# First expert tile's weights split, rows turned and first two product groups made during self-attention's last tiles

## What is computed

```
x = x + cross_attention(layernorm(x), ctx)        # 16 heads of 32
x = x + self_attention(layernorm(x))              # latent keys and values, rope, 16 heads
x = x + experts(layernorm(x))
experts: w, idx = top_k(xf @ Wr, 2); w = softmax(w)
         h = xf @ W1[e]; g = xf @ W3[e]; y = (silu(h) * g) @ W2[e]     # e of 8, hidden 768
         out = sum over the two chosen experts of w * y
```

## Time and profile before

| | us |
|---|---|
| median of three runs (lowest, highest) | 1528.22 (1528.01, 1528.5) |
| the profiled execution's own time | 1529.74 |
| its span, first to last instruction | 1528.0 |
| PE busy | 1446.4 (95%) |
| DVE busy | 1084.5 (71%) |
| ACT busy | 808.3 (53%) |
| POOL busy | 542.2 (35%) |

### The profile page before, as it was taken

The page is one execution under the profiler, slowest core; times in us unless marked ns, Lnnn a source line. Parts: engine busy times, 40 slices in busy tenths (PEclk is TensorE's granted clock), DMA queues, the critical chain, the costliest instruction groups (busy, mean ns, idle before and its releaser), DMA issues. The chain is left out here.

```text
span 1528.0 us, 39476 instructions
## 1 busy us (share of the span) xinstructions
PE 1446.4 (95%) x14944; PEld 1291.2 (85%) x14944; DVE 1084.5 (71%) x1939; ACT 808.3 (53%) x1527; POOL 542.2 (35%) x816
## 2 busy tenths in 40 slices
PE   7999999999999999987999997689999999999997
PEld 6888888888888888776777776589999999999996
DVE  4667767777777767745567676587877888787784
ACT  4666666666666666544334332245555555555552
POOL 1222222222222222215857776432342333333232
PEclk9999999999999999999999999699999999999999
DMA  6310101001100100100011015068878778787871
GB/s 233 127 29 23 29 28 28 24 25 28 28 28 21 28 28 22 29 1 2 30 37 37 31 37 174 30 216 262 280 251 287 252 248 269 265 280 238 286 244 42
DMA packets 130734, 174.10 MB, mean 114 GB/s; under 512 B 16954, under 2 KB 89338, under 8 KB 130627
## 3 DMA queue, kind: packets, MB, share of 16 engines
q1 hardware_dynamic: 120242, 145.56, 29.5%
q0 software_dynamic: 10384, 27.05, 4.9%
HBM read 157.18 MB, written 19.06 MB: 115 GB/s over the span
## 5 line engine op out<-in xcount | busy, mean ns | idle before, releaser
L2071 DVE TENSOR_TENSOR lo<-raw,hi 128x1024 fp32r<-128x1024 f32 x207 | 246.0, 1219 | 8.2 <-ACT hi L2007 6.6
L52 PE MATMUL mo_bank<-xT_hi,hi 128*128 128x256 f32 x768 | 217.2, 283 | 3.2 <-DVE xT_lo L2080 2.8
L54 PE MATMUL mo_bank<-xT_lo,hi 128*128 128x256 f32 x768 | 216.0, 281 | 0.0
L53 PE MATMUL mo_bank<-xT_hi,lo 128*128 128x256 f32 x768 | 216.0, 281 | 0.0
L2007 ACT CAST hi<-raw 128x1024 fp32r<-128x1024 f32 x207 | 208.3, 1048 | 6.8 <-DMA raw<-in_L_ffn_W_dram 4.0
L590 ACT ACTIVATE Pr<-xa_s,nmax 128x257 f32<-128x257 f32 x256 | 118.8, 472 | 124.3 <-DVE nmax L686 124.2
L2027 ACT ACTIVATE sl<-mo_bank 128x256 f32<-128x256 f32 x117 | 44.9, 384 | 248.4 <-PE mo_bank L54 248.4
L52 PEld LDWEIGHTS mo_bank<-xT_hi,hi 128*128 128x128 f32 x768 | 145.8, 190 | 9.7 <-issue 5.6
L52 PE MATMUL xa_s<-zT_hi,QK_hi 128*128 128x258 f32 x512 | 151.7, 296 | 1.9 <-DVE zT_lo L618 1.9
L53 PEld LDWEIGHTS mo_bank<-xT_hi,lo 128*128 128x128 f32 x768 | 145.6, 190 | 3.3
L54 PEld LDWEIGHTS mo_bank<-xT_lo,hi 128*128 128x128 f32 x768 | 145.8, 190 | 0.0
(11 more groups left out here) (307 smaller groups left out, 3968.1 us busy)
## 6 DMA issues: line engine op xcount, KB each, us to landing
raw<-in_L_ffn_W_dram SPq DMA_DIRECT2D x207, 512.0 KB, 5.8
raw<-in_ctx_dram SPq DMA_DIRECT2D x64, 256.0 KB, 2.6
out_dram<-x_res SPq DMA_DIRECT2D x16, 256.0 KB
xs<-xn SPq DMA_DIRECT2D x16, 256.0 KB
x_res<-in_x_dram SPq DMA_DIRECT2D x1, 3584.0 KB, 19.0
VL<-v_last_rows SPq DMA_DIRECT2D x128, 2.0 KB, 1.5
raw_o<-in_L_xattn_Wo_dram SPq DMA_DIRECT2D x1, 1024.0 KB, 6.2
raw_q<-in_L_xattn_Wq_dram SPq DMA_DIRECT2D x1, 1024.0 KB, 9.4
```

The source lines that it names most:

```text
L52: pe.matmul(out, lh, rh, start=start, stop=False)
L53: pe.matmul(out, ll, rh, start=False, stop=False)
L54: return pe.matmul(out, lh, rl, start=False, stop=stop)
L2071: vW.done(dve.tensor_tensor(lo, raw, hi.bitcast(F32), ALU.subtract), f"p{c}{q}")
```

## The change

- Split weights and turned rows of the first expert tile get memory that lives through both blocks (`Held`); cross-attention's and self-attention's temporary tensors share it. PSUM banks (`Banks`) and the experts' step counters (`ExpertSteps`) are shared by both blocks too.
- In self-attention ACT splits (0,0) and (0,1) before `exponent(13)`, and (0,2), (1,0), (1,1) ahead of `normalise_again(13)`; DVE makes the other halves of (0,0) and (0,1) in step 13, (0,2) behind `logits(14)` and (1,0) at the very end.
- POOL gathers the rows before `power` of tile 13. PE turns them behind the scores of tile 15 and ahead of `turn_again(13)`, and makes HG0 ahead of `project(14)` and HG1 ahead of the last `ranks`. DVE's half of the turned rows stands between `softmax_end(14)` and `softmax_start(15)`.
- The list of the first rows is loaded before the row store of tile 12. Six token tiles are sent in the tail and two instead of four in the experts' block.
- Experts: the first tile starts with `silu` of group 0 and its Y0. `pick` moves behind DVE's step j = 0, `fill` is cut in six parts, behind j = 1 to 5 and behind `add_share`. SP loads slot 0 of the second tile before it waits for the sends.

```diff
@@ self-attention: SP
+                    if i == n_tile - 4:
+                        sp.wait_ge(stored, 16 * i)
+                        sp.wait_ge(sent_early, 32 * n_early)
+                        first_tile.load_places(sp)
                     aN2.wait(sp, i, "xn")
                     sp.dma_start(xs_t[i], xn2[:]).then_inc(stored, 16)
...
-                    if i == n_tile - 4:
-                        sp.wait_ge(stored, 16 * (i + 1))
-                        sp.wait_ge(sent_early, 32 * n_early)
-                        first_tile.load_places(sp)
@@ self-attention: PE, ranks and the tail
+                    if g in late_groups:
+                        vA.wait(pe, n_tile - 1, "add")
+                        vR.wait(pe, g - 1, "cnt")
...
+                def turn_first():
+                    pe.wait_ge(first_tile.x_got, 32)
+                    vG.wait(pe, a - 2, "lg")
+                    vA.wait(pe, a - 1, "add")
+                    for c, bank in enumerate((b_lat, b_qo)):
+                        for k in range(KC):
+                            mm = pe.transpose(bank[:, k * P:(k + 1) * P], first_tile.xg[:, c, k * P:(k + 1) * P], ident[:])
+                    flow.pX.done(mm, "XT")
+
+                def first_hg(j, bank):
...
+                    flow.vX.wait(pe, 0, "0x1")
+                    flow.vW.wait(pe, 0, "p01")
+                    if j == 1:
+                        vB.wait(pe, b, "sub")
...
                 scores(a, b_s)
+                scores(b, b_turn)
+                turn_first()
                 turn_again(a - 1)
-                scores(b, b_turn)
                 weighted(a)
                 gate(a - 1)
+                first_hg(0, b_lat)
                 project(a)
                 weighted(b)
                 project(b)
                 turn_again(a)
+                ranks(len(groups) - 2)
                 gate(a)
-                ranks(len(groups) - 2)
                 turn_again(b)
                 gate(b)
+                first_hg(1, b_turn)
                 ranks(len(groups) - 1)
@@ self-attention: ACT
                 for i in range(n_tile - 2):
+                    if i == n_tile - 3:
+                        first_split(0, 0)
+                        first_split(0, 1)
                     exponent(i)
...
+                pK.wait(act, b, "done")
+                first_split(0, 2)
+                pQ.wait(act, b, "done")
+                first_split(1, 0)
+                first_split(1, 1)
+                normalise_again(a - 1)
                 exponent(a)
-                normalise_again(a - 1)
+                first_turned()
                 turned_again(a - 1)
@@ self-attention: DVE
                     softmax_end(i)
+                    if i == n_tile - 3:
+                        first_split(0, 0)
                     latents(i + LEAD)
...
                     turn_heads(i + 1)
+                    if i == n_tile - 3:
+                        first_split(0, 1)
                     attended(i)
...
+                turn_heads(b)
                 softmax_start(a, b_s)
-                turn_heads(b)
                 softmax_end(a)
+                first_turned()
                 softmax_start(b, b_turn)
...
+                place(len(groups) - 2)
                 logits(a)
-                place(len(groups) - 2)
+                first_split(0, 2)
                 logits(b)
                 choose(len(groups) - 1, (0, 1))
                 place(len(groups) - 1)
+                first_split(1, 0)
@@ self-attention: POOL
+                first_tile.gather(pool, n_early * P)
                 power(vN2, gN2, aN2, a - 1, mvb, rstdb, shiftb)
-                first_tile.gather(pool, n_early * P)
-                pPV.wait(pool, a, "done")
-                send(8)
+                for j in range(n_early, n_early + 4):
+                    send(j)
                 power(vN2, gN2, aN2, a, mvb, rstdb, shiftb)
-                pPV.wait(pool, b, "done")
-                send(9)
                 power(vN2, gN2, aN2, b, mvb, rstdb, shiftb)
-                for j in range(10, late_from):
+                for j in range(n_early + 4, late_from):
                     send(j)
@@ experts: SP
                     for c in range(NS):
                         vW.wait(sp, index(t, pos) - 1, f"p{c}2")
                         slots[c].load(sp, W1, W3, W2, e)
+                        if between is not None and c == 0:
+                            sp.wait_ge(sent, 32 * (n_tile - 8))
+                            between()
@@ experts: PE
-                turn(0, 0, True)
...
                     for j in range(NH):
-                        hg(t, pos, j)
+                        if not first or j >= PAIR:
+                            hg(t, pos, j)
@@ experts: ACT
-                split(0, 0, 0, 0)
-                split(0, 0, 0, 1)
-                x_hi(0, 0)
-                split(0, 0, 0, 2)
...
-                        splits(t, pos, j, last)
+                        splits(t, pos, j, last, ((1, 0), (1, 1)) if first else ())
@@ experts: DVE
-                split(0, 0, 0, 0)
-                split(0, 0, 0, 1)
-                x_lo(0, 0)
-                split(0, 0, 0, 2)
-                tiles.pick(dve, count, 1)
...
-                        splits(t, pos, j, last)
-                        if first and 1 <= j <= tiles.FILL_PARTS:
+                        splits(t, pos, j, last, ((1, 0),) if first else ())
+                        if first and j == 0:
+                            tiles.pick(dve, count, 1)
+                        elif first:
                             tiles.fill(dve, count, j - 1)
                     add_share(t, pos)
                     splits(t, pos, NH, last)
+                    if first:
+                        tiles.fill(dve, count, NH - 1)
@@ experts: POOL
                 for i in range(late_from, n_tile):
                     send(i)
+                gather_x(0, 1)
                 gather_acc(0, 0)
-                gather_x(0, 1)
                 gather_x(0, SINGLE)
                 scatter_acc(0, 0)
@@ perceiver_block
-    late_from = n_tile - 4
+    late_from = n_tile - 2
```

208 lines of the change are left out of this document (137 added, 71 removed).

## The result

In 20 runs of each kernel the changed kernel took 1531.82 us at the median (1528.46 to 1536.08), the one before 1528.16 (1523.81 to 1531.83). The ratio is 1.0023, with an interval of 1.0013 to 1.0032: slower by 0.23%, some 3.6 us, where I had forecast 0.7 us less. That lies just inside my range of 1521.5 to 1532, but on the other side of no change. The profiled execution took 1533.08 us with a span of 1531.2.

A forecast was written before the change was run, and what follows sets the result against it. DVE was taken as the bound for one tile behind the meeting, short chained steps ahead of it, PE in the steady part. -7.3 + 2.5 + 4.1 = -0.7 us gave 1527.5 us, range 1521.5 to 1532.

The forecast's parts named there:

- part 3: Self-attention's tail: the work moved there makes the meeting 4.1 us later, bounds -0.6 and 6.9.
- the meeting: Point between self-attention and experts where the engines go on; at 984.97 before, forecast near 989.
- I had 2.2: HG1 ahead of the last ranks, at the low clock: a cost of 2.2 us, bounds 0 and 2.4.
- The split (1,0): DVE's last weight split, behind the final place at the tail's end: a cost of 1.1 us.
- the gather, the turn and HG0: Work put into the chain of self-attention's last two tiles: a cost of 0.8 us, between -1.7 and +3.4.
- Case D: Rival, chance 0.08: first rows land late, at 957.3, holding up PE and DVE 4.6 us; 1532.1 us.
- Part 1: Behind the meeting: Y0 of the experts' second tile comes earlier, a gain of 7.3 us, upper end 10.4.
- B: Time of the meeting, from which the prediction counts: 984.97 before, forecast to move by 4.1 us.
- the landing of slot 0: Second tile's weight load: lands 10.2 us after its issue, costing DVE 3.1 us of waiting.
- Part 2: Experts' second tile: the late table delays the third tile's loads, a loss of 2.5 us, between 0 and 6.7.
- a cover of 1.7 us: Slack left between the late scatter and row gather landing and the add_share that follows them.
- Case A: The forecast itself, chance 0.47: real gain behind the meeting, mostly given back by late table and later meeting; 1527.5 us.

The follow-up runs named there:

- e5: The changed kernel run again with no edit, in the second series on its own chip: 1524.14 us, 0.9976 of the kernel before.
- f12: The changed kernel with no edit, as control of the fourth series on another chip: 1524.43 us, 0.9965 of the kernel before.
- e7: The changed kernel with the table in its early place and HG1 made behind the meeting: 1519.9 us, 0.9945 of the kernel before.
- e4: The changed kernel with the table filled behind j = 1 to 5, nothing behind add_share: 1521.86 us, 0.9945 of the kernel before.
- e6: The changed kernel with POOL's tail sends paced as before and the table early: 1521.7 us, 0.9955 of the kernel before.
- e10: The changed kernel with POOL's gather of the first rows back behind the tail's first power: 1532.91 us, 1.0029 of the kernel before.
- e11: The changed kernel with the table early and both HG0 and HG1 made behind the meeting: 1530.01 us, 1.0005 of the kernel before.
- g17: Same kernel as e7, run again in the fifth series: 1525.74 us, 0.9989 of the kernel before.
- g18: The changed kernel with all 128 matmuls of scores(8) issued twice: 1538.15 us, 1.0051 of the kernel before.
- g19: The changed kernel with 64 matmuls of scores(8) issued twice, in the fifth series: 1531.7 us, 1.0020 of the kernel before.
- e1: The changed kernel with POOL's tail sends again waiting for weighted(14) and weighted(15): 1528.0 us, 0.9983 of the kernel before.
- e3: The changed kernel with turn_again(13) put back between the scores of tiles 14 and 15: 1525.32 us, 0.9974 of the kernel before.
- f14: Same kernel as e3, run again in the fourth series: 1526.81 us, 0.9981 of the kernel before.
- g16: The changed kernel with no edit, as control of the fifth series: 1532.01 us, 1.0017 of the kernel before.

## Why the prediction was wrong

**The step that failed is part 3, ahead of the meeting.** I had the meeting later by 4.1 us (bounds -0.6 and 6.9); after showed 10.15. The prediction saw the one gap marked "issue" of the kernel before, 2.84 us in weighted(14), and took it as gone; it gave PE's supply of instructions no price. I had weighted(14) done at 957.0; in after it starts at 965.59, and what stands between is scores(15), trickling from 955.0 to 961.95. Compared with e5, 9.1 us are lost up to the turn of the first rows; 3.9 of them come back up to the turn of the last tile's `xn`, 2.4 of these because HG0 then runs at the higher clock (2.9 us against 5.3). The stretch from there to the meeting is 1.0 longer.

**Without the shortage the term was right as a whole, in part by luck**: 42.34 - 38.35 = 3.99 us in e5, 3.71 in f12. Its parts, from rows of e5 and of e7:

```profile
965.13 0.42 PE L52 MATMUL bank<-sa_wo_hi,sa_OT_hi 128*128 128x512 f32 x1
...
968.04 1.29 PE L1028 MATMUL bank_four<-Pt,Vt 32*32 32x32 f32 x128
...
978.99 1.88 PE L1038 MATMUL bank_four<-sa_wr,xn2T 128*128 128x8 f32 x8 [0.67 <-ACT xn2T L1200]
...
985.84 0.30 PE L1053 MATMUL bank<-both,below 128*128 128x24 f32 x2
```

```profile
983.39 0.18 DVE L1390 TENSOR_TENSOR both<-pick_all 128x16 f32<-128x16 f32 x1
...
987.12 0.17 DVE L1422 CAST idx<-rows 128x4 uint32<-128x4 f32 x1
987.20 1.22 DVE L1444 TENSOR_TENSOR split<-raw,split 128x1024 fp32r<-128x1024 f32 x1
```

```profile
978.04 0.62 PE L1053 MATMUL bank<-both,below 128*128 128x24 f32 x2 [2.74 <-DVE both L1389]
```

These are PE and DVE of e5, then PE of e7. Where `ranks` waits for DVE in e7, in e5 it stands behind HG1: `both` is there at 983.57 and `ranks` starts at 985.84, 2.3 us late. I had 2.2. Since the clock is up by then, `ranks` itself is shorter (0.30 against 0.62 us), and the net of HG1 is 1.7 us; between e7 and e4 the stretch from the turn of the last `xn` to the meeting differs by 1.8. The split (1,0) I had at 1.1 us with no cover. From `idx` to the meeting it was 1.05 us before and is 1.41 in e5, so it costs 0.4. That POOL's last sends cover the rest is likely, but was not tried. The rest is 4.0 - 1.7 - 0.4 = 1.9 us for the gather, the turn and HG0, where I had 0.8 and the upper bound 3.4. I had reckoned this term at the end of project(14), and there e5 is 3.0 us behind, near that bound: it ends at 968.04 in e5 and at 965.26 before, with scores(14) 0.26 us earlier. weighted(14) was done at 958.1 instead of 957.0. HG0 ran at the lower clock (5.3 us, 959.86 to 965.13), but project(14) ran at the higher one (2.9 us, 965.13 to 968.04); I had them both low or both high. Then 1.6 us came back up to the turn of the last `xn`, since project(15) ran at the higher clock, where before the granted clock was 0.57 in 968 to 972. 0.5 us went again in that turn and the last gate (1.88 against 1.38 us). No term of mine held this return.

**The gather.** Case D wanted the rows at 956.5 or later; the turn could start at 953.57 in e5 (952.7 forecast), so D did not come. POOL was free for it at 946.03 in e5 instead of 944.88, and my 952.7 held nothing of the 0 to 1.6 us that I had named for this. Two rows of e5's POOL show why, beside the 1.28 of such a row before, with the two splits of DVE next to them:

```profile
934.97 1.18 DVE L1444 TENSOR_TENSOR split<-raw,split 128x1024 fp32r<-128x1024 f32 x1
935.74 1.54 POOL L1526 TENSOR_TENSOR part_cos<-qraw,rope_t 128x512 f32<-128x512 f32 x1 [1.31 <-DVE Pt L1342]
...
938.77 1.46 DVE L1444 TENSOR_TENSOR split<-raw,split 128x1024 fp32r<-128x1024 f32 x1
939.22 2.14 POOL L1539 TENSOR_TENSOR qr<-part_cos,part_sin 128x512 f32<-128x512 f32 x1
```

Together they are 1.1 us longer than 2 x 1.28, within the 0 to 1.6, and short of the 2.3 that I drew from the rule of the Trainium skill ("SBUF — State Buffer", section "SBUF: two separate sides"). The rows don't speak against the exclusion: only 0.4 us of the first split and 1.0 us of the second lay beside these rows, and my 2.3 took both splits as wholly beside POOL's work.

**Part 1** was forecast at -7.3 and was -9.75: Y0 of the second tile starts at B + 36.35. The first `a_lo` came at B + 2.92 (2.95 forecast). The term that was off is the landing of slot 0. I had it land 10.2 us after its issue, and 3.1 us of waiting; it was issued at 1002.69 and used at 1010.41, 7.7 us, and ACT waited 0.95.

**Part 2** was forecast at +2.5. From Y0 of the second tile on, after gives back 9.75 - 6.16 = 3.6 us, and against e4 the late table costs 4.56 (2.3 between e5 and e6). ACT's wait for slot 0 of the third tile is there (3.63 us), but PE loses only 0.38 and 0.89 us by it. The rest is what I had as a cover of 1.7 us. It held for the first tile's sums. It failed one step later: the next gather of rows, late by the table, now stands on POOL just ahead of the next scatter. In after the scatter starts at 1056.45, 2.7 us after DVE began to add that tile's sums (1053.71); before it was 1.6 us (1051.72 to 1053.31). The first two rows are POOL's in after, the third is POOL's before:

```profile
1054.25 0.95 POOL L2287 DMA_INDIRECT xg<-xs,of_row  x1 [0.30 <-issue]
1056.45 1.84 POOL L2303 DMA_INDIRECT out_dram<-acc,of_row  x1 [0.16 <-POOL e_carrier L2272]
...
1053.31 1.84 POOL L2186 DMA_INDIRECT out_dram<-acc,of_row  x1 [0.56 <-POOL e_carrier L2155]
```

With the longer issue of the `acc` gather behind it, DVE waits 4.80 us where it was 2.38, and PE 1.65 and 0.69. I had written that with the cover gone every us is one of PE, and then did not price it.

**The sum** without the shortage is 3.99 - 6.91 = -2.9 us in e5 (tail, and 143.80 against 150.71 behind the meeting) and 3.71 - 6.90 = -3.2 in f12. Their spans are 3.0 and 4.2 us below that of before, their medians 4.6 and 5.7 us below. So my -0.7 was too high by 2 to 5 us for a series without the shortage, and too low by 4.4 for the first comparison. Both signs were measured for one and the same program. Case A did not come as I forecast it in either; its form (a real gain behind the meeting, given back by the table and the meeting) is what the profiles show, with the shortage on top.

**What stays open.** What makes the gaps. It is shown that they are there or not by series (each on its own chip), in profiles that have the same program. The unpaced sends, the early gather, the late table and both HGs do not bring them by themselves: e5 and f12 have all of these and no gaps. The gather's old place, the early table, the tail without the HGs and a shift of PE's list do not end them (e10, e11, g17, g18, g19). Pacing was run only where there are none (e1, e6), so whether it would end them is not known. The order with turn_again(13) between the scores (e3, f14) was run only in series without them either, so whether parting the two runs of small matmuls would help is not known. Nor is it known why the kernel before is spared. Its list has turn_again(13) between the two scores, as e3 and f14 have, and scores(15) starts 5.7 us after scores(14) (3.5 in e5). Its own gap of 2.84 us comes after 128 matmuls of scores(15) (124 in the row below, four more between those of weighted(14)) and 29 of weighted(14) in a row:

```profile
946.62 1.29 PE L996 MATMUL sa_pv<-Kt,Qt 32*32 32x32 f32 x128
...
952.34 1.88 PE L996 MATMUL sa_bank<-Kt,Qt 32*32 32x32 f32 x124
```

That fits a supply that two such runs close together outpace, but it is an argument, not a result.

## What to carry to other kernels

A gap marked "issue" in the profile before is a resource with no name in the sum; when work is moved next to it, give it both ends of a range instead of taking it as gone. Work that lets something be ready "just in time" (here the last part of the table) must be priced through each queue behind it, on to the next tile: of PE's 3.6 us of gaps, only 1.3 was the wait that I had looked for. And when an edit that doesn't touch a stretch makes that stretch 7 us shorter, run the unedited kernel again beside it before believing in any of the edits. The version to keep is that of e7: table in its early place, HG0 early, HG1 behind the meeting, 0.9945 and 0.9923 where there is no shortage and 0.9989 (to 1.0004) where there is.

## What the runs showed of the hardware

In a stretch with 16 KB loads of instructions at 947.0, 951.5, 956.0 and 962.0 (e5, in steps of 0.5 us), PE ran 128 matmuls of 32x32 with their weight loads in 1.5 us; with none starting from 955 to 964 (g16) it still went on, at five matmuls in about 0.74 us. That is about a twelfth of the rate, not a stop, and the full rate came back (961.72 in g16) some 3 us ahead of the next load (in the step from 964.5). The same program showed it in three comparisons (1.0017 to 1.0042) and not in two others (0.9965 and 0.9976); four of them were on four different chips, and the chip of the first comparison is not on record. A comparison of two kernels within half a percent can therefore turn its sign with the series.
